# An attention layer over a graph: one of every three groups, in place of four, has a tile's keys and values made from picked columns, and the first gathers wait differently

## The reference

```python
Q_h = (x @ Wq + bq).reshape(N, H, D)          # N = 6250, H = 8, D = 12
K_h = (x @ Wk + bk).reshape(N, H, D)
V_h = (x @ Wv + bv).reshape(N, H, D)
E = (edge_attr @ We + be).reshape(-1, H, D)   # 100000 edges
src = K_h[src_idx]
dest = Q_h[dst_idx]
score = src * dest / jnp.sqrt(jnp.asarray(D, x.dtype)) * E
score = jnp.exp(jnp.clip(score.sum(-1, keepdims=True), -5.0, 5.0))
msg = V_h[src_idx] * score
wV = jax.ops.segment_sum(msg, dst_idx, num_segments=N)
Z = jax.ops.segment_sum(score, dst_idx, num_segments=N)
h_out = wV / (Z + 1e-06)
x = _layernorm(x + h_out.reshape(N, 96))
```

## Time and the profile before

| what | value |
|---|---|
| median of three runs | 1252.93 us (1249.06 to 1254.93) |
| the profiled execution | 1249.5 us, of which the span from first to last instruction is 1247.7 us |
| mean granted clock of TensorE | 0.81 |
| gathers | 36 early ones and 700 from the table |
| columns copied | 2944 on ScalarE, 2944 on VectorE |
| first L886 of the loop, last | 98.08 us, 1230.18 us: 196 groups |

### The profile page before, as it was taken

One profiled execution on the slowest core, in us unless ns is written; L12 is line 12 of the kernel. 1 busy time (PEld: TensorE's weight loads), 2 busy tenths in 40 slices (PEclk: granted clock), 3 DMA queues, 4 the chain that ended last, 5 costly groups with the idle time before them and its releaser, 6 DMA issues.

```text
span 1247.7 us, 24998 instructions
## 1 busy us (share of the span) xinstructions
PE 840.3 (67%) x3571; PEld 489.7 (39%) x3571; DVE 817.4 (66%) x4620; ACT 743.1 (60%) x4040; POOL 697.4 (56%) x744
## 2 busy tenths in 40 slices
PE   6555676676676767668666676677667667577765
PEld 4442343343343444334333344344344334343344
DVE  6013676776776777767667676777667667656658
ACT  3225666666676666667656665666666566666653
POOL 5725655556555556565565565565565656555560
PEclk9667888888978778987888778777787888787786
DMA  9914444444444444443444444444444444444430
GB/s 246 266 41 132 120 114 114 119 121 116 116 125 113 112 115 121 133 117 107 118 131 113 109 117 120 113 126 118 110 122 113 123 115 116 111 120 116 115 89 24
DMA packets 122307, 149.25 MB, mean 120 GB/s; under 512 B 57071, under 2 KB 90623, under 8 KB 122132
## 3 DMA queue, kind: packets, MB, share of 16 engines
q0 software_dynamic: 34736, 70.56, 22.3%
q1 hardware_dynamic: 87088, 76.15, 21.7%
q10 hardware_dynamic: 310, 0.87, 0.2%
HBM read 137.51 MB, written 9.98 MB: 118 GB/s over the span
## 4 chain that ended last, share of the span: by engine, by line
issue 46%; POOL 29%; DVE 9%; PE 5%; DVEq 3%; another core or an unknown queue 2%; ACT 2%; DMA 2%; POOLq 0%; ACTq 0%; SPq 0%
POOL kv L592 29%; DVE early_t L1036 3%; DVEq L429 1%; DVE qe_t L886 1%; DMA kv<-kv_table,src_idx 1%; DVE node_stage L878 1%; DVE kq L903 1%; ACT early_t L705 1%; PE ps_eq L1199 1%; DVEq L1026 1%; PE ps_eq L1206 1%; DVE ps_last L910 1%; DVE node_stage L924 1%; DMA w_all<-biases_in 1%
## 5 line engine op out<-in xcount | busy, mean ns | idle before, releaser
L592 POOL DMA_INDIRECT kv<-kv_table,src_idx x700 | 661.3, 945 | 504.4 <-DVE qe_t L886 201.0
L705 ACT COPY early_t<-x_t 97x1 f32 x2944 | 309.8, 189 | 108.5 <-issue 104.6
L1036 DVE COPY early_t<-x_t 97x1 f32 x2944 | 215.7, 143 | 134.5 <-issue 126.1
L1199 PE MATMUL ps_eq<-ea,w_all 128*96 128x512 f32 (+1 forms) x262 | 174.0, 752 | 119.6 <-DVE qe_t L886 98.9
L1206 PE MATMUL ps_eq<-pick_t,q_win 128*96 128x512 f32 (+1 forms) x262 | 178.4, 771 | 61.3 <-ACT e_t L729 42.4
L723 ACT ACTIVATE pick_t<-distance 80x512 f32<-80x512 bf16 x196 | 123.2, 629 | 153.4 <-remote 98.9
L910 DVE TENSOR_REDUCE ps_last<-kq 128x32 f32<-128x384 f32 x196 | 108.7, 554 | 77.6 <-issue 46.5
L715 ACT ACTIVATE distance<-rel_bc,neg_part 80x512 bf16<-80x512 bf16 x196 | 138.8, 708 | 12.9 <-issue 12.6
L1242 PE MATMUL ps_qe_seg<-node_stage 128*104 128x80 f32 x784 | 107.4, 291 | 49.6 <-remote 34.4
L1199 PE MATMUL ps_eq_qe<-ea,w_all 128*96 128x512 f32 x130 | 87.3, 760 | 72.5 <-DVE qe_t L886 48.7
L1242 PEld LDWEIGHTS ps_qe_seg<-node_stage 128*104 128x104 f32 x784 | 99.2, 207 | 54.3 <-issue 50.9
(11 more groups left out here) (97 smaller groups left out, 885.0 us busy)
## 6 DMA issues: line engine op xcount, KB each, us to landing
ea<-ea_t_in SPq DMA_DIRECT2D x196, 192.0 KB
rel_bc<-rel_rows_dram SPq DMA_DIRECT2D x196, 80.0 KB
kv<-kv_table,src_idx POOLq DMA_INDIRECT x700
q_win<-q_table SPq DMA_DIRECT2D x196, 30.0 KB
kv_table<-node_stage SPq DMA_DIRECT2D x5, 576.0 KB
x_t<-x_t_in SPq DMA_DIRECT2D x5, 480.0 KB, 9.2
node_stage<-x_rows_in SPq DMA_DIRECT2D x11, 192.0 KB
out<-node_stage SPq DMA_DIRECT2D x11, 192.0 KB
```

The costliest lines, as they stand in the source:

```text
L592: pool.indirect_dma_start(rows[0:n, :], None, table, bass.IndirectOffsetOnAxis(ap=src_idx[0:n, tile:tile + 1], axis=0)).then_inc(semaphore ...
L705: last = nc.scalar.copy(staged(local, row), column)
L1036: last = nc.vector.tensor_copy(staged(local, row), column)
L1199: nc.tensor.matmul(ps_eq[2 * group % 3][0:DIM, 0:n], w_e, ea[:, slot, 0:n], start=True, stop=True).then_inc(e_e, 1)
```

## The change

A local tile now comes once in three groups in place of four: 62 of them (groups 11, 14, ..., 194). Its 128 columns are picked in 3 rounds, 22 in each by ScalarE and 21 by VectorE (20 in the last). ScalarE gets a function addresses like VectorE's: the addresses of the first 8 columns are made behind L723 and ahead of L729, the second load has 14 numbers, and their addresses are made ahead of the copies. The early gathers wait less for the tables: gather i waits until t_mm has reached 5i/4 - 13. The first 15 gathers from kv_table (groups 9 to 12) get a wait that they did not have, for the early products: the first waits until x_mm is 4, each further one for one more, up to 18.

```diff
93.43 0.48 ACT L679 COPY kv<-ps_eq 128x384 f32<-128x384 f32 x1 [0.17 <-PE ps_eq L1175] -77,12 +77,13 93.43 0.48 ACT L679 COPY kv<-ps_eq 128x384 f32<-128x384 f32 x1 [0.17 <-PE ps_eq L1175]
 FINAL_RING = 3
 KV_RING, EA_RING, REL_RING, QWIN_RING, PICK_RING, MSG_RING = 16, 8, 8, 8, 4, 4
 QE_RING = 3
-TABLES_BEHIND = 3
+EARLY_UNPACED = 13
+PRODUCTS_AHEAD, PACED_BY_PRODUCTS = 4, 13 * GROUP_TILES
 LEAD_FIRST, LEAD_LEAST, LEAD_FALLS_EVERY = 13, 4, 8
 GENERAL, WINDOWED, STREAMED = 0, 1, 2
-PICK_ROUNDS, COLS_ACT, COLS_DVE, LOADED = 4, 16, 16, 16
+PICK_ROUNDS, COLS_ACT, COLS_DVE, LOADED = 3, 22, 21, 24
 ON_ACT = PICK_ROUNDS * COLS_ACT
 LOCAL_T = GROUP_TILES - 1
 PICK_FIRST, LOCAL_SETTLE, LOCAL_LEAD, STAGED = 2, 3, 3, 8
93.43 0.48 ACT L679 COPY kv<-ps_eq 128x384 f32<-128x384 f32 x1 [0.17 <-PE ps_eq L1175] -601,14 +602,17 93.43 0.48 ACT L679 COPY kv<-ps_eq 128x384 f32<-128x384 f32 x1 [0.17 <-PE ps_eq L1175]
             def gather_early(groups):
                 for group in groups:
                     for t in range(GROUP_TILES):
-                        made = min(group * GROUP_TILES + t - TABLES_BEHIND, TABLE_TILES // 2)
+                        made = min((group * GROUP_TILES + t) * 5 // 4 - EARLY_UNPACED, TABLE_TILES // 2)
                         if made > 0:
                             pool.wait_ge(t_mm, made)
                         room_for(group * GROUP_TILES + t)
                         gather(kv[:, group, t, 0:DIM], x_rows, group, t, landing_of(group, t))
-            def keep_pace(round_, t):
-
+            def keep_pace(group, t):
+
+                round_ = group - lead(group)
+                if group * GROUP_TILES + t < PACED_BY_PRODUCTS:
+                    pool.wait_ge(x_mm, min(2 * EARLY, PRODUCTS_AHEAD + (group - EARLY) * GROUP_TILES + t))
                 if t == 1 and round_ >= ADDED:
                     pool.wait_ge(e_acc, round_ - ADDED + 1)
                 if t == 2 and round_ + 1 >= 0:
93.43 0.48 ACT L679 COPY kv<-ps_eq 128x384 f32<-128x384 f32 x1 [0.17 <-PE ps_eq L1175] -629,7 +633,7 93.43 0.48 ACT L679 COPY kv<-ps_eq 128x384 f32<-128x384 f32 x1 [0.17 <-PE ps_eq L1175]
                     if group >= KV_RING:
                         pool.wait_ge(e_msg, group - KV_RING + 1)
                     for t in range(gathered_tiles(group)):
-                        keep_pace(group - lead(group), t)
+                        keep_pace(group, t)
                         room_for(gathered_before(group) + t)
                         gather(kv[:, slot, t, :], kv_table, group, t, landing_of(group, t))
93.43 0.48 ACT L679 COPY kv<-ps_eq 128x384 f32<-128x384 f32 x1 [0.17 <-PE ps_eq L1175] -694,6 +698,11 93.43 0.48 ACT L679 COPY kv<-ps_eq 128x384 f32<-128x384 f32 x1 [0.17 <-PE ps_eq L1175]
                     return []
                 return columns_of(mybir.EngineType.Activation, local, round_, first, end - first)
+            def addresses(columns):
+
+                for column in columns:
+                    act.lower_ap(column)
+
             def copy_columns(group, picked):
                 local, round_ = pick_round(group)
93.43 0.48 ACT L679 COPY kv<-ps_eq 128x384 f32<-128x384 f32 x1 [0.17 <-PE ps_eq L1175] -774,9 +783,12 93.43 0.48 ACT L679 COPY kv<-ps_eq 128x384 f32<-128x384 f32 x1 [0.17 <-PE ps_eq L1175]
                     picked = columns(group, 0, COLS_ACT // 8 * 4)
                     if group + TURNED + 2 < GROUPS:
                         make_pick_t(group + TURNED + 2)
+                    addresses(picked)
                     if group + TURNED + 1 < GROUPS:
                         copy_features(group + TURNED + 1)
-                    picked += columns(group, COLS_ACT // 8 * 4, COLS_ACT)
+                    rest = columns(group, COLS_ACT // 8 * 4, COLS_ACT)
+                    addresses(rest)
+                    picked += rest
                     copy_columns(group, picked)
                     if group < GROUPS:
                         exponentials(group)
```

## The result

Kernel after: 1259.57 us (median of 12 runs, 1255.45 to 1264.40); kernel before, beside it: 1253.53 us (12 runs, 1249.06 to 1258.34). The ratio is 1.0046 (95% interval 1.0026 to 1.0065): no gain, but a loss of 6 us, small and clear of the noise. The forecast was 1232, a gain of 21. The range of 1200 to 1298 holds the time; the kernel did not get faster.

The account below looks back on a forecast made before the run. It took a steady 1.63 to 1.65 us per gather, with stalls behind runs of gathers, as the pace. From 1249.5 us: gathers -26, columns +22, products +3, first gathers -19 gave 1229.5, 1232 on the runs' scale; range 1200 to 1298.

Parts of the forecast that it names:

- ScalarE's addresses: Between L723 and ScalarE's first copy: up to 0.8 us wait a group, hidden by the gathers, costed 0; uncovered 149 us.
- the sum: Whole kernel: 1249.5 - 26 + 22 + 3 - 19 = 1229.5 us, given as 1232 on the scale of the runs.
- what the prediction named last as able to upset it: Loop: the constant price per gather is chance; groups are bound by their own work plus stalls.
- Gathers: Loop: 16 gathers fewer at 1.64 us each save 26 us; low end 0.
- Columns: Loop: 6 more copies per group on ScalarE, 5 on VectorE, cost 22 us; bounds 0 to 104.
- The gap: ScalarE, before a group's first column copy: idle up to 0.8 us behind load and addresses.
- First gathers: Prologue: new waits let early products end near 75 us, not 93.9, saving 19 us; bounds 0 and 25.
- ScalarE becomes the pace: Rival, between L723 and first L705 of each group: ScalarE's cycle plus stalls passes 6.0 us; 1285 us, chance 0.34.
- Its other signs: For ScalarE as pace: 1.80 us per gather and above, GpSimd waiting for L886 at most gathers.
- The second rival, rarer stalls: Loop: slower groups ask for gathers less densely, price falls to 1.54 us; 1198 us, chance 0.12.
- The new waits do nothing: Rival, prologue: tables stall under denser gathers, the 19 us go; 1251 us, chance 0.12.

Follow-up runs that it names:

- chip B: Any of three chips on which the kernel before takes 947 to 948 us and hardly stalls.
- chip A: The chip with stalls: kernel before takes 1238 us at one time, 1251 at another; the first measurement is counted with it by its times.
- five rounds by threes: Kernel before with new waits, one tile of every fifth group, 13 and 13 columns, ScalarE's addresses by threes: 954.69 us, ratio 1.0081.

## Why the prediction was wrong

*The step that failed* is in the part on ScalarE's addresses: "What hides it now is the pace of the gathers: ScalarE's own cycle goes from at most 3.77 to about 3.77 + 0.56 + 0.8 = 5.1, and 3.67 gathers at 1.64 are 6.0. I cost it at 0". It took 1.64 us per gather for a floor under which 5.1 us of ScalarE would lie. The floor did not hold: with stalls, the profile after has 1.77 us per gather in the stretch that had 1.65 before, and its chain is on ScalarE and its sequencer for 55% of the span. Taken bare, on a chip B, the addresses ahead of the copies cost 107 us. What they cost on chip A was not measured: the changed kernel with the addresses at each copy ran there only with its loads split. By the sum the loop should have got 1 us shorter (26 off, 22 and 3 on). It got 25.7 us longer in the first trace; of this 12.6 were won back in front of it.

The price per gather was the time of a group divided by its gathers: work of the engines plus stalls. The floor that gathers really set is the 1.24 of a chip B. There the prediction's way of hiding does work, as long as the group's own work stays under it: with 13 columns the addresses cost nothing that shows, with 22 and the load of 14 they cost 107 us. This is what the prediction named last as able to upset it.

*Gathers* were mis-sized by the same mistake: 26 us predicted, 18.5 measured on a chip B, where they are at GpSimd's own pace. With stalls they weren't measured alone.

*Columns*, 22 us: with the longer loads they cost 68 us on a chip B, where 104 was the bound. On chip A the term isn't measured alone either. The gather instruction shows nothing of VectorE's copies: in the kernel before, from 100 us on, it takes 945 ns in the mean of the 78 that run beside ten or more column copies of VectorE, and 944 in the mean of the 355 that run beside none; in the changed kernel 947 and 946. The Trainium skill says in SBUF — State Buffer, section "SBUF: two separate sides", that 32-bit copies of VectorE in a two-port mode lock GpSimd out of its port; the traces do not show that for these copies of one column.

*The gap* was put at up to 0.8 us and is 1.05, about what the load of 14 numbers adds, which takes 1.26 in place of 0.98.

*First gathers*: the mechanism was right. The size was 12.6 us in the first trace in place of 19, but that trace is the latest of five. With the new waits and stalls the first product of the loop comes at 77.7, 80.0, 81.0, 81.6 and 85.5 us, with the old waits at 98.1 and 98.7; the forecast was 79. In the first trace the early gathers ended at 53.16 + 0.95, not near 50 (two breaks of 2.80 and 1.23 us stayed), and nine groups of products took 22.6 us from the first copy to the last, not 19; new gathers start at 61.73, in the middle of them. Without stalls it is worth 3 to 4 us.

*The rivals.* "ScalarE becomes the pace" was right in its place, the gap, which is there in full. It got 0.34. Its range, 1255 to 1320, holds the time, but its sum of 1285 is 25 us too high. Its other signs came by half. The time per gather lies between the two cases (1.66 to 1.77, where up to 1.70 was the forecast and from 1.80 this rival), and 155 gathers waited for L898, against 110 for L886 before: most groups, not most gathers. The second rival, rarer stalls, came true beside it and not in its place: 0.41 us a group less stands still. That is the larger part of why a change that costs 153 us on chips B costs 6 to 9 with stalls. Against the kernel before, the changed one stands still 0.41 us a group less with stalls; on a chip B, against the waits alone, it stands 0.12 more. The rest grows by 0.54 and 0.71. All told, a chip with stalls adds 291 to 306 us to the kernel before (1238.1 and 1253.5 against 947.5), but 147 to 159 to the changed one (1247.2 and 1259.6 against 1100.4). "The new waits do nothing" did not hold; that its range of 1240 to 1260 holds the time too is luck.

*The sum* was off by 1 us as written: 1229.5 and 3.4 are 1232.9, not 1232. Nothing hangs on it.

*Still open.* What causes a stall, and what it has to do with the granted clock. The unit of 0.7 us is seen; the count of instructions as its only ration is excluded; a run that removes gathers alone on chip A was not made. Whether a gap placed in ScalarE takes stall time away, because GpSimd is asked more sparsely, or only lies at the same time as a stall, is argued from the table, not shown.

*A better version.* On chip A the old columns with the new waits and addresses by threes beat both kernels (0.986), on chips B the waits alone do (0.996). The waits alone on chip A, and loads of 12 and 12 numbers, were not tried.

## What to carry to other kernels

A quotient that stays the same over several stages (time per gather) is no floor until something shows the engine busy at that pace; ask what the engine does back to back (here 1.25 us) and call the rest unexplained. A gap made on an engine that has no slack between stalls is a cost even if stalls now cover it: cost it bare and covered, and let the range say so. Before you put a price on one of several changes in a run, subtract what the others cost: five rounds by threes took 10.6 us more than the waits alone, and nine gathers account for 11. Registers are loaded by the number: look how long a load of the new length and offset takes before you lengthen or split it.

## What the runs showed of the hardware

- A load of node numbers from SBUF into registers is not proportional to its length. Medians of single instructions, counted from the traces, for numbers from an offset that is a multiple of four: 4 in 0.32 us, 8 in 0.55, 9 in 0.79, 11 in 1.23, 14 in 1.26, 16 in 1.12, 20 in 1.39, 21 in 1.63. From offset 11, 11 numbers take 2.44, and from offset 13, 8 numbers 1.9. Fours cost about 0.28 and each number beside them 0.22 to 0.24, and from these two odd offsets every number costs that: an estimate that fits all of these.
- The same program takes 947 us on three chips and 1238 to 1253 with stalls. GpSimd's gather instruction is 944 to 949 ns on both, VectorE's column copy 140 to 144, a matmul 358 and 399. Of the 1.44 us a group between them (4.37 with the waits alone, 5.81 before) 1.08 is time in which nothing starts.
- In a stall single instructions of ScalarE's and SyncE's sequencers take about 0.7 us, also waits that are long satisfied, and column copies are spaced by as much.
- Where nothing stalls GpSimd issues one gather of 128 rows each 1.25 us, with 32 column copies a group as with 26 (197 and 196 in 244.4 us).
